# Where the residual is added: in the output by an accumulating scatter, or on GpSimd from rows that carry it

## The reference, cut to what matters

```python
x = x + xattn(layernorm(x), ctx, ...)
h = layernorm(x) * gamma + beta
shared_out = silu(h @ sw1.T) @ sw2.T
probs = softmax(h @ router_w.T)
top_prob, top_idx = max(probs), argmax(probs)
routed_out = silu(h @ ew1[top_idx].T) @ ew2[top_idx].T * top_prob
out = x + shared_out + routed_out
```

## Time and profile before

| | |
|---|---|
| median of 3 runs | 825.51 us (825.13 to 829.35) |
| the profiled execution | 822.83 us, span 821.0 us |
| TensorE, VectorE, ScalarE, GpSimd busy | 674.1, 640.7, 586.1, 578.7 us |
| attention stage | to about 690 us of the span |
| first transpose of a tile, last one | 694.97, 795.49 us |

### The profile page before, as it was taken

How to read it: one execution, slowest core, us unless ns; L and a number is a source line. 1 busy time by engine, 2 the same in 40 slices (tenths; PEclk the granted TensorE clock), 3 DMA queues, 4 the chain that set the end, 5 groups by cost and what they waited for, 6 DMA issues and landing times.

```text
span 821.0 us, 22257 instructions
## 1 busy us (share of the span) xinstructions
PE 674.1 (82%) x7738; PEld 471.7 (57%) x7738; DVE 640.7 (78%) x1411; ACT 586.1 (71%) x1324; POOL 578.7 (70%) x684
## 2 busy tenths in 40 slices
PE   3689779899989998999889898989997555777883
PEld 2355546666666666666656565766664343655652
DVE  3878768889888988788888888888977647676873
ACT  3668667888787878788787878787876622665662
POOL 1356557787878778697888787878877755365664
PEclk9989999999999999999999999999998877899997
DMA  7289867898998998979998889999795913699991
GB/s 256 39 170 161 174 125 151 167 172 184 171 173 169 167 180 170 187 156 181 175 175 166 162 172 170 175 179 177 138 165 136 165 45 119 129 143 142 149 132 15
DMA packets 367523, 126.87 MB, mean 155 GB/s; under 512 B 331114, under 2 KB 362740, under 8 KB 367412
## 3 DMA queue, kind: packets, MB, share of 16 engines
q1 hardware_dynamic: 359604, 116.11, 74.2%
q0 software_dynamic: 7232, 8.79, 7.2%
q10 hardware_dynamic: 576, 0.54, 0.2%
HBM read 30.71 MB, written 14.71 MB: 55 GB/s over the span
## 4 chain that ended last, share of the span: by engine, by line
PE 31%; DVE 20%; issue 14%; DMA 11%; SPq 9%; ACT 8%; POOL 6%; DVEq 0%; ACTq 0%; POOLq 0%
PE FB L358 10%; DMA pt<-p_split 8%; PE TBK L1463 4%; DVE neg_max L1208 4%; PE S L1391 4%; SPq L514 4%; POOL p_split L582 3%; ACT p_split L784 2%; DVE FB L946 2%; SPq L507 2%; DVE above L951 2%; ACT k_st L747 2%; DVE v_st L976 2%; DVE hn L1058 2%; SPq L508 2%
## 5 line engine op out<-in xcount | busy, mean ns | idle before, releaser
L582 POOL TENSOR_TENSOR p_split<-probs,p_split 128x512 f16<-128x512 f32 x256 | 300.6, 1183 | 62.8 <-ACT p_split L784 60.2
L822 ACT ACTIVATE probs<-S,neg_max 128x512 f32<-128x512 f32 x256 | 175.3, 685 | 16.1 <-DVE neg_max L1208 14.8
L784 ACT ACTIVATE p_split<-probs 128x512 f16<-128x512 f32 x256 | 161.1, 629 | 16.0 <-DMA pt<-p_split 14.5
L1208 DVE TENSOR_REDUCE neg_max<-S 128x1 f32<-128x512 f32 x256 | 171.1, 679 | 0.3
L358 PE MATMUL FB<-xt_hi,w_split 128*128 128x256 f16 x768 | 141.6, 276 | 3.2 <-DVE xt_lo L973 2.9
L1407 PE MATMUL O<-v_st,pt 128*128 128x64 f16 x1024 | 114.8, 195 | 23.0 <-DMA pt<-p_split 22.9
L1407 PEld LDWEIGHTS O<-v_st,pt 128*128 128x128 f16 x1024 | 93.3, 99 | 56.4 <-DMA pt<-p_split 32.8
L1408 PE MATMUL O<-v_st,pt 128*128 128x64 f16 x1024 | 114.1, 194 | 0.0
L1409 PE MATMUL O<-v_st,pt 128*128 128x64 f16 x1024 | 114.1, 194 | 0.0
L1391 PE MATMUL S<-k_st,q_st 64*128 64x512 f16 x768 | 107.1, 385 | 1.1 <-ACT probs L822 1.1
L358 PE MATMUL FB<-xt_lo,w_split 128*128 128x256 f16 x384 | 105.8, 276 | 0.0
(11 more groups left out here) (223 smaller groups left out, 1752.4 us busy)
## 6 DMA issues: line engine op xcount, KB each, us to landing
w_raw<-in_L_ffn_expert_w SPq DMA_DIRECT2D x16, 512.0 KB, 4.4
w_split<-rows SPq DMA_DIRECT2D x39, 132.0 KB, 2.5
c_in<-in_ctx SPq DMA_DIRECT2D x16, 256.0 KB
x_in<-in_x SPq DMA_DIRECT2D x16, 256.0 KB
xb<-in_x SPq DMA_DIRECT2D x16, 256.0 KB, 3.3
pt<-p_split SPq DMA_TRANSPOSE x256, 3.3
out<-rest SPq DMA_DIRECT2D x15, 256.0 KB, 2.7
k_st<-in_L_xattn_Wk SPq DMA_DIRECT2D x2, 512.0 KB, 7.1
```

What stands on the lines that cost most here:

```text
L582: g.tensor_tensor(p_split[n % HL_RING][:, 1, :], probs[n % PROBS_RING][:, :], p_split[n % HL_RING][:, 0, :], ALU.subtract).then_inc(p_lo_r ...
L784: a_(p_split[g % HL_RING][:, 0, :], probs[g % PROBS_RING][:, :], ACT.Copy).then_inc(p_hi_ready, 1)
L822: a_(probs[n % PROBS_RING][:, :], S[n % 4][:, :], ACT.Exp, bias=neg_max[:, n % 4:n % 4 + 1], accum_out=sums[:, n % UNITS:n % UNITS + 1]).t ...
L1208: v.tensor_reduce(neg_max[:, n % 4:n % 4 + 1], S[n % 4][:, :], AX.X, ALU.max, negate=True)\
```

## The change

A row of `rows` gets a second half of 264 floats, which holds the token's residual: 2112 bytes instead of 1056. VectorE and GpSimd build the residual in `row` itself instead of in `rest`, and the store of the residual to `out` goes away. The row scatters carry it along. For the last sequence the first halves are scattered as before, and the second halves in two scatters of their own once the last residual is there. In the expert stage the ring has 8 places of double size instead of 16. For the first 8 tiles SyncE loads the first halves and GpSimd the second ones; from tile 8 on SyncE loads whole rows. `scale_out` raises a new semaphore `e_y`; GpSimd adds the residual to each `e_res`, raises `e_out`, and scatters the sum of the tile before plainly to `out`. TensorE waits for `e_y` where it waited for `e_out`; SyncE's loads wait for `e_out` still.

```diff
-RING = 16
+RING = 8
-WIDTH = D + 8
+HALF = D + 8
-EARLY_COUNT, EARLY_RANKS, EARLY_PLACE, EARLY_SCATTER = 40, 41, (42, 43), 44
+EARLY_COUNT, EARLY_RANKS, EARLY_PLACE, EARLY_SCATTER = 40, 41, (42, 43), 46
...
     (SyncE, attention stage)
-                t = due(n, STORE_R)
-                if t is not None and t < B - 1:
-                    sp.wait_ge(r_ready, t + 1)
-                    sp.dma_start(out_v[t], rest[t % 2][:, :, :]).then_inc(r_stored, 16)
...
             def load_rows(a):
                 at = sp.value_load(tile_row[0:1, bass.ds(a, 1)], min_val=0, max_val=E * ROOM - P)
-                sp.dma_start(g_rows[a % RING], rows[bass.ds(at, P), :]).then_inc(row_in[a % RING], 16)
+                cols = HALF if a < RING else 2 * HALF
+                sp.dma_start(g_rows[a % RING][:, 0:cols], rows[bass.ds(at, P), 0:cols]).then_inc(row_in[a % RING], 16)
...
-                sp.dma_start(rows[bass.ds(at, P), :], zeros).then_inc(padded, 16)
+                sp.dma_start(rows[bass.ds(at, P), :].rearrange("p (k c) -> p k c", k=2), pad_rows).then_inc(padded, 16)
...
                     if a + LEAD >= RING:
+                        if a + LEAD == RING:
+                            sp.wait_ge(r_scattered, 16 * TB)
                         sp.wait_ge(e_out, a + LEAD - RING + 1)
                     load_rows(a + LEAD)
                 turn_tile(a)
...
     (GpSimd)
+            def scatter_last_heads():
+                pool.wait_ge(placed, B * 2)
+                g.tensor_scalar(half_at[:, 0, :], dest[:, :], 2.0, None, ALU.mult).then_inc(halves_ready, 1)
+                g.tensor_scalar(half_at[:, 1, :], dest[:, :], 2.0, 1.0, ALU.mult, ALU.add).then_inc(halves_ready, 1)
...
+                for i in range(TB):
+                    scatter(row[(B - 1) % 2][:, i, 0:HALF], half_rows, half_at[:, 0, i:i + 1], 2 * E * ROOM - 1)\
+                        .then_inc(h_scattered, 16)
...
-                    r = rest[t % 2][:, :, :]
+                    r = row[t % 2][:, :, HALF:HALF + D]
                     g.tensor_tensor(r, r, x2[t % 2][:, :, :], ALU.add).then_inc(r_ready, 1)
...
             pool.wait_ge(r_ready, B)
-            g.dma_start(out=out_v[B - 1], in_=rest[(B - 1) % 2][:, :, :]).then_inc(last_r_stored, 16)
-            pool.wait_ge(r_stored, 16 * (B - 1))
-            pool.wait_ge(last_r_stored, 16)
-            for a in range(SLOTS):
-                pool.wait_ge(e_id, a + 1)
-                pool.wait_ge(e_out, a + 1)
-                g.indirect_dma_start(out=out, out_offset=bass.IndirectOffsetOnAxis(ap=slot_idx[:, a:a + 1], axis=0),
-                                     in_=e_res[a % OUTS], in_offset=None, bounds_check=B * T - 1, oob_is_err=False,
-                                     compute_op=ALU.add).then_inc(stored[a % OUTS], 16)
+            pool.wait_ge(halves_ready, 2)
+            for i in range(TB):
+                scatter(row[(B - 1) % 2][:, i, HALF:2 * HALF], half_rows, half_at[:, 1, i:i + 1], 2 * E * ROOM - 1)\
+                    .then_inc(r_scattered, 16)
+            pool.wait_ge(tiles_ready, 1)
+            pool.wait_ge(padded, 16 * E)
+            pool.wait_ge(scattered[0], 16 * TB * (B // 2))
+            pool.wait_ge(scattered[1], 16 * TB * (B // 2 - 1))
+            pool.wait_ge(r_scattered, 16 * TB)
+            for a in range(RING):
+                at = pool.value_load(tile_row[0:1, a:a + 1], min_val=0, max_val=E * ROOM - P)
+                g.dma_start(out=g_rows[a][:, HALF:2 * HALF], in_=rows[bass.ds(at, P), HALF:2 * HALF]).then_inc(rest_in[a], 16)
+            for a in range(SLOTS + 1):
+                if a < SLOTS:
+                    if a < RING:
+                        pool.wait_ge(rest_in[a], 16)
+                    pool.wait_ge(row_in[a % RING], 16 * (a // RING + 1))
+                    pool.wait_ge(e_y, a + 1)
+                    g.tensor_tensor(e_res[a % OUTS], e_res[a % OUTS], g_rows[a % RING][:, HALF:HALF + D], ALU.add)\
+                        .then_inc(e_out, 1)
+                if a > 0:
+                    pool.wait_ge(e_id, a)
+                    pool.wait_ge(e_out, a)
+                    scatter(e_res[(a - 1) % OUTS], out, slot_idx[:, a - 1:a], B * T - 1).then_inc(stored[(a - 1) % OUTS], 16)
...
     (VectorE)
-                    dve.wait_ge(r_stored, 16 * (t - 1))
-                v.tensor_tensor(rest[t % 2][:, :, :], tb2, shared_row[:, :].unsqueeze(1).broadcast_to([P, TB, D]),
+                    dve.wait_ge(scattered[t % 2], 16 * TB * (t // 2))
+                v.tensor_tensor(row[t % 2][:, :, HALF:HALF + D], tb2, shared_row[:, :].unsqueeze(1).broadcast_to([P, TB, D]),
...
-                                       ALU.mult, ALU.mult).then_inc(e_out, 1)
+                                       ALU.mult, ALU.mult).then_inc(e_y, 1)
...
     (TensorE, down)
-                    pe.wait_ge(e_out, a - 1)
+                    pe.wait_ge(e_y, a - 1)
```

More of the change, by code:

```diff
@@ L77 @@
 COUNT_AT = 42
-DOWN_AT, ADD_R, STORE_R = 44, 46, 47
+DOWN_AT, ADD_R = 44, 46
 SCATTER_AT = (53, 55)
@@ L165, in xattn_ffn @@
         hn = sb("hn", [P, TB, D], F32)
-        row = [sb(f"row{i}", [P, TB, WIDTH], F32) for i in range(2)]
-        rest = [sb(f"rest{i}", [P, TB, D], F32) for i in range(2)]
+        row = [sb(f"row{i}", [P, TB, 2 * HALF], F32) for i in range(2)]
+        half_at = sb("half_at", [P, 2, TB], U32)
         ht = sb("ht", [P, TB, 2 * DC, P], F16)
@@ L268, in xattn_ffn @@
         scattered = [sem(f"scattered{i}") for i in range(2)]
-        r_stored = sem("r_stored")
-        last_r_stored = sem("last_r_stored")
+        halves_ready = sem("halves_ready")
+        h_scattered = sem("h_scattered")
+        r_scattered = sem("r_scattered")
+        rest_in = [sem(f"rest_in{i}") for i in range(RING)]
         zeroed = sem("zeroed")
@@ L362, in xattn_ffn @@
         c_v = ctx_in.rearrange("b (t p) d -> b p t d", p=P)
-        out_v = out.rearrange("(b t p) d -> b p t d", p=P, t=TB)
+        half_rows = rows.rearrange("n (k c) -> (n k) c", k=2)
         ew1_v = ew1.rearrange("e (c p) d -> e p c d", p=P)
@@ L400, in xattn_ffn @@
         pad_at = piece(E).bitcast(I32)
-        zeros = under[:, :].bitcast(F32)[:, 0:WIDTH]
+        zeros = under[:, :].bitcast(F32)[:, 0:HALF]
+        pad_rows = zeros.unsqueeze(1).broadcast_to([P, 2, HALF])
         iota_tile = x_in[:, 0, 0:SLOTS]
@@ L547, in _ @@
             for a in row:
-                g.memset(a[:, :, D:WIDTH], 0.0).then_inc(const_ready, 1)
+                for half in range(2):
+                    g.memset(a[:, :, half * HALF + D:(half + 1) * HALF], 0.0).then_inc(const_ready, 1)
             g.iota(expert_down[:, :], [[-1, E]], base=E, channel_multiplier=0,
@@ L845, in _ @@
                         at = act.value_load(pad_at[0:1, e:e + 1], min_val=0, max_val=E * ROOM - P)
-                        nc.scalar.dma_start(rows[bass.ds(at, P), :], zeros).then_inc(padded, 16)
+                        nc.scalar.dma_start(rows[bass.ds(at, P), :].rearrange("p (k c) -> p k c", k=2), pad_rows).then_inc(padded, 16)
                 if n == LAST_T + UP_AT[1] + 2:
```

24 lines of the change are left out of this document (15 added, 9 removed).

## The result

The changed kernel takes 861.92 us (median of 4 runs, 857.14 to 864.33) beside 827.36 us for the kernel before on the same chip (825.13 to 829.35): a ratio of 1.041, 95% interval 1.035 to 1.047. Slower, as forecast, but 18 us above the forecast of 844 us and outside its range. The forecast stood on 825.5 us for the kernel before, so against that kernel it said +19 us, and the medians differ by 34.6 us. The profiled execution took 860.92 us.

A forecast was written before the change was run, and what follows sets the result against it. The prediction took SyncE's queue to pace the expert stage's tiles. Its terms, 13.4 + 6.0 - 0.3 = +19.1 us, put on a median of 825.5 us, gave 844 us, with a range of 832 to 858 us.

The forecast's parts named there:

- What bounds the kernel: Expert stage: SyncE's queue paces the tiles at 2.73 us each; the DMA engines' load adds some tenths to latencies.
- The attention stage: Attention stage: row scatters cost by their 128 rows, not by bytes, so the stage is unchanged, 0 us.
- The move: Before the last counting: sequence 14's cast and scatters, now directly ahead of it, come whole into the path, +3.4 us.
- The pads: Pad writes before the first tile: doubled size costs nothing because GpSimd is later; without that cover 1 to 2 us.
- GpSimd's way into the stage: Expert stage's start: residual scatters, eight loads and first addition delay tile 6's transpose by 13.4 us, the 3.4 us included.
- The ring in steady state: Tiles 6 to 36: three tiles per round take 6.6 + 0.9 + 1.3 = 8.8 us against 8.2, +6 us.
- The end: After the last tiles: GpSimd's extra work, shorter latency and sooner landing of plain scatters together give -0.3 us.
- Rival 2: Expert stage: the round stays at today's full-load latency, 9.8 us, +16 us, or 855 us; chance 0.12.
- Rival 3: Attention stage: scatters cost by bytes, 1 us more for each of 28, +14 us, 858 us; chance 0.05.
- Rivals 1 and 4: First: only the expert stage's entry costs, 838.6 us, chance 0.16; fourth: GpSimd's queue runs ahead, 822 us, chance 0.05.

The follow-up runs named there:

- e8: The kernel before with the two early row scatters of sequence 14 moved behind the residual addition, nothing else; 834.5 us, ratio 1.003 to the kernel before.
- e12: The changed kernel, ring of 8, with no residual loaded, GpSimd still adding, and pads written in one half; 849.5 us, ratio 1.022 to the kernel before.
- e1: The changed kernel with a ring of 16 places instead of 8; 843.1 us, ratio 1.016 to the kernel before.
- e5: The changed kernel with a ring of 9 places instead of 8; 845.3 us, ratio 1.016 to the kernel before.
- e7: The kernel before with a plain scatter to `out` instead of the accumulating one, residual left out; 828.3 us, ratio 0.997 to the kernel before.
- e3: The changed kernel without GpSimd's loads of second halves for the first eight tiles, their residual left out; 856.2 us, ratio 1.032 to the kernel before.
- e2: The changed kernel with SyncE loading only first halves from tile 8 on, their residual left out; 857.3 us, ratio 1.030 to the kernel before.
- e11: The changed kernel with half loads from tile 8 on, SyncE's loads waiting for VectorE's result instead of GpSimd's addition; 846.0 us, ratio 1.017 to the kernel before.
- e4: The kernel before with a ring of 8 instead of 16 and nothing else; 842.7 us, ratio 1.014 to the kernel before.

## Why the prediction was right in its direction and wrong in its size

- **What bounds the kernel.** Right for the kernel before. With the change SyncE waits for GpSimd's addition, as forecast, and its share of the chain fell to 2%.
- **The attention stage at 0.** Right as far as the profiles tell: 1.042 us per scatter, and the counting of sequence 14 lies in the same range with and without the change.
- **The move, +3.4.** Right: 2.9 us at T(0) by e8, and 3.0 in the median.
- **The pads at nothing, 1 to 2 without cover.** Wrong for T(0): 3.2 us by e12. The cover held at T(6) alone. There GpSimd was the later one, as the text said, so this cost disappears in the changed kernel and appears as soon as the ring lifts the wait (e1, e5).
- **GpSimd's way into the stage, T(6) +13.4.** Right: +11.8 us from the common point (+6.2 to T(0) and +5.6 behind it), in part because two errors offset each other. The second residual scatter started 34.3 us behind the counting of sequence 14, where the forecast had 32.4, 1.9 us late. From there to the end of the eight loads it took 13.2 us for the 16.5 forecast, since a load took 1.16 us and not 1.6. The landing was taken at 3.7 us, the median of the kernel before; the two residual scatters landed after 2.6 and 3.0 us. The Trainium skill, page "DMA: Bandwidth & Descriptors", section "Anatomy of one DMA", gives by its fit an estimate of 2.3 us from issue to landing for these bytes. The trace lies between that and the forecast's 3.7 us, nearer to the page; over all of its indirect scatters the changed kernel has a median of 3.7 us.
- **The ring in steady state, +6: the step that failed.** The mechanism is as forecast: rounds of three tiles, released by GpSimd's addition. The size of the round is not. Of "6.6 + 0.9 + 1.3 = 8.8 us for three tiles", the 0.9 holds, the 1.3 is 1.2 at the least and 1.5 by the mean, and the latency was 7.9 and not 6.6: together the measured round of 10.2 us and +20 us in ten of them. The text had a row at 7.4 us and took a value near that of the entry, 6.5 us, the shortest of the whole trace, on the ground that "the DMA engines are relieved too" and that doubled loads take "some of it back". The relief does shorten the latency, as far as one profile tells: 7.1 us in e7 for 7.4 and 7.9. But nothing of the relief was left: with a ring of 8 the latency is 7.9 and 7.7 us with doubled loads (the changed kernel, e3) and 6.9, 7.0 and 7.4 us with half loads (e2, e11, e12). And the forecast had no term for TensorE's clock, which fell as soon as the tiles came in threes: without the lower clock the latency is 7.0 us, nearer to the 6.6, and with it 8.2. The upper bound, +17, was passed as well, since it too was made of single rows for the latency, without their spread; e4, where the rounds take 9.4 us and the sum of the parts says 8.7, speaks for a cost of the spread itself.
- **How the +20 divides.** Ring of 8 alone: 93.5 for 82.0 to 84.5, about +9 to +11 (e4). Doubled loads with that ring: 102.2 for 93.9 (e2), about +8; but e12, with half loads too, stands at 97.4, which makes it +5, and the spread is nearly as large. GpSimd's addition: 93.9 for 91.9, about +2 and within the spread (e11). They are not independent: none costs more than the spread with 16 places, and nine are nearly as good.
- **The end, -0.3.** Measured +2.3: the plain scatter gives 2.8 us (28.2 to 25.4, e7), so additions and loads take about 5. The sum itself had a slip: 2.3 for 1.86 us over five tiles is 2.2 us more and not 1.6.
- **The rivals.** Rival 2, the round at 9.8 us and 855 us, came nearest by its mechanism and had 0.12; its reason, that the latency does not fall, is what happened. Rival 3 was nearest by its number, 858 us, and by that alone: its cause is out by the scatters' 1.042 us. Rivals 1 and 4 are out by the pace and by T(6).

What stays open: why the same kernel spreads its pace by some 3 us between profiles, and how much of the 10.2 us round is owed to TensorE's clock, of which below.

## What to carry to other kernels

Before a ring is made shorter, work out its round and divide it by the number of tiles that fit in it. Here the round goes from a transpose, through every step, to the transpose that waits for its result. Of the 8 places two are taken by the loads ahead and three by the steps that VectorE's last one lies behind, so three tiles fit in a round, and with 9 places four. If the quotient is not clearly below the pace of the issuing engine, the kernel pays, and in e4 it paid more than the means say; one place more took the ratio from 1.041 to 1.016 here. The gaps that a short ring makes can also lower TensorE's clock (0.84 in the changed kernel, 0.98 with 16 places), and a step of TensorE then took 3.3 us for 1.8. A low busy share of the DMA engines is no sign of a short latency: at 0.66 it was 7.9 us here, and at 0.94 it had been 7.4.

## What the runs showed of the hardware

- An indirect scatter of 128 rows costs GpSimd the same for 1056 and 2112 bytes per row (1.039 and 1.042 us). One to `out` that accumulates costs 1.63 us by the median of its largest group, a plain one 1.04, and the software queue took 36.3% of the engines' time for 4.47 MB with it, 12.3% for 4.92 MB without.
- The four pad writes as two copies of a buffer in each row take 5.67 us on SyncE for 3.92. The issue itself became longer: 0.56 us for 0.34 by the median.
- TensorE's clock fell where the tiles came in threes. In the changed kernel the stretches of 5 us from 730 to 805 us stand at 0.66 or at 1.00, mostly in turn: the engine runs at 1.2 GHz for a part of each round, after the gap in which it waited for a transpose. In the kernel before every such stretch from 715 to 810 us stands at 1.00, and with nine or 16 places T(6) to T(36) stands at 0.94 to 1.00. TensorE is busy 71.8 us for 65.5 with the same matmuls.
- By the latencies of 7.9 us over all and 7.0 us without the lower clock, it would add up to 0.9 us to a round, an estimate from these two means. Against so much speaks e3: its clock stands at 0.93, TensorE is busy 68.9 us, and it has nearly the same pace (100.5 us). No run here changes the clock alone, and a fall of the clock is itself a consequence of the waits: the ring of 16 brought it back to 0.98.
